# A mixture-of-experts tail that scatters its tokens to sorted rows, against one that gathers each tile inside the loop

## The chip, the cores and the metric

The kernel runs on one core of a Trainium2 chip. The time is that of the device in microseconds, the median of three runs: 3569.94 us (3564.78 to 3572.04). Engines are named as the profile names them: PE (TensorE), DVE (VectorE), ACT (ScalarE), POOL (GpSimd) and SP (SyncE). SP does no arithmetic here; it issues transfers. POOL issues transfers too, the indirect ones (gathers and scatters by a list of rows) among them.

## The reference

One decoder layer on x of 4 x 1024 tokens of width 256, in fp32. Every part adds to x and normalises:

```
x = layernorm(x + attn(x))      # a Mamba block twice (state 16, inner 512), then a decaying memory
x = layernorm(x + xattn(x, ctx))  # 16 heads over 64 context rows
x = layernorm(x + ffn(x))       # the part that the change is about

ffn(x):  logits = x @ Wg + bg                       # 8 experts
         top2, idx = top_k(logits, 2); scores = softmax(top2)
         y_e = gelu(x @ W1[e] + b1[e]) @ W2[e] + b2[e]   # hidden 1024
         out = sum over the two chosen e of score * y_e
         return layernorm(x + out) * gamma + beta
```

## The kernel before, in words

The five engines run own instruction streams and wait on each other by counting semaphores. The first three quarters of the time are the scan of the Mamba blocks and, in two groups of two batches, memory and cross-attention (xattn). At the end of xattn a batch's result (x2, 8 tiles of 128 tokens, 1 MB) stands in `x2_out`, which is also the place of the last batch in `x2`. SP stores batches 0 to 2 in `x2_dram` (`keep_x2`) as they are done.

The expert part begins when the last layer norm is done (`ln_done`). SP loads batch 0 (`x2_first`) and batches 1 and 2 (`x2_middle`). PE turns x2 (`turn_x2`, drained by ACT) and forms the logits (`logits`), for batches 0 and 3 first, then for 1 and 2. DVE routes: the two largest of 8 logits, one-hot selections, a count of the tokens ahead of each by two matrix products with `below` and `ones`, and from these `slot`, the row of each (token, choice) in a list sorted by expert. Each expert's part of the list begins on a tile of 128 rows (`bound`, in tiles). With 4096 tokens and two choices there are at least `FEWEST` = 64 tiles and at most `TILES` = 80; here there are 70.

When `slot` is known (`routed`), POOL issues 64 indirect stores (2 choices x 32 tiles of tokens), which write rows of x2 to `xs_dram` in sorted order. When all have landed (`xs_sorted`), SP loads the first sorted tile into `tile_in`. `xs_dram` is filled with zeros at the very start of the kernel, as are the upper tiles of `ys_dram`, so that rows without a token are defined.

The tile loop runs over expert pairs and, in each expert, over its tiles. One pass of PE does: the first product (two halves of 512 columns) of tile i+1; the transposes of tile i's hidden values (`turn_hidden`); the transposes of tile i+2 from `tile_in` (`turn_tile`); the second product of tile i. DVE adds b1 and b2 and copies turned values, ACT does gelu and drains. SP, in a loop of its own, waits until tile i+1 has been turned (`tileT_full`) and loads the next into the same `tile_in`; there is one such buffer. POOL (`keep_results`) waits for tile i's result (`y_ready`) and stores it in `ys_dram`; after the last tile of an expert it issues the four loads of the weights of the expert after next (`load_expert`, 2.6 MB) into the buffer that has come free. The first two experts' weights are issued right after `ln_done`.

At the end POOL gathers each token's two results from `ys_dram` by `slot`, and DVE weighs, adds and normalises, batch by batch.

`alone(engine)` is a step without work that separates two waits from the instruction after them. The transfers of one issuing engine stand in one queue: q1 in the profile for SP, q0 for POOL.

Of the kernel before, what the change touches and what calls it, by code (L numbers as in the profile page):

```python
# [38 lines left out]
def decoder_layer(nc, x, ctxT, ctx_mask, norm1_w, norm2_w, in_wT, in_b, conv_w, conv_b, xp_wT, dt_wT, dt_b,  # L39
# [57 lines left out]

    with ExitStack() as ctx:
# [11 lines left out]
        x2_dram = nc.dram_tensor("x2_dram", (NT - TT, P, D), F32, kind="Internal").ap()  # L110

        xs_dram = nc.dram_tensor("xs_dram", ((TILES + 1) * P, D), F32, kind="Internal").ap()
# [50 lines left out]
        WORDS = 41552  # L163
# [68 lines left out]
        tile_in = carve(D)  # L232
# [7 lines left out]
        tileT = carve(KD * P).rearrange("p (k t) -> p k t", k=KD)  # L240

# [3 lines left out]

        hid, act_hid = small[:, 0:HID], small[:, HID:2 * HID]
# [10 lines left out]
        steps_i = read_w_sb[:, 1, :].bitcast(I32).rearrange("p (e j) -> p e j", e=E)  # L257
        count = read_w_sb[:, 0, 0:E]
# [84 lines left out]
        xs_sorted = sem("xs_sorted")  # L343
# [132 lines left out]
        batch_order = [0, B - 1] + list(range(1, B - 1))  # L476
# [34 lines left out]
        ZEROED = 16 * (-(-(TILES + 1) // 4) + (TILES - FEWEST) // 4)  # L511
# [16 lines left out]
        def _(sp):  # L528
# [30 lines left out]
            for g0 in range(GROUPS):  # L559
# [22 lines left out]
                for u in range(2):  # L582
# [22 lines left out]
            sp.dma_start(x2[:, 0:TT, :], x2_dram[0:TT].rearrange("t p d -> p t d")).then_inc(x2_first, 16)  # L605
            sp.dma_start(x2[:, TT:NT - TT, :], x2_dram[TT:NT - TT].rearrange("t p d -> p t d")).then_inc(x2_middle, 16)

            sp.wait_ge(xs_sorted, 16 * 2 * NT)
            sp.wait_ge(routed, 1)
            sp.dma_start(tile_in, xs_dram[0:P, :]).then_inc(xs_loaded, 16)  # L610
            tiles = sp.value_load(bound[0:1, E:E + 1], min_val=FEWEST, max_val=TILES)
            with sp.Fori(0, tiles) as i:

                sp.wait_ge(tileT_full, i + 2)
                sp.wait_ge(xs_loaded, i * 16 + 16)
                alone(sp)
                sp.dma_start(tile_in, xs_dram[bass.ds(i * P + P, P), :]).then_inc(xs_loaded, 16)
# [1266 lines left out]
```

## Time and profile before

| | |
|---|---|
| median of 3 runs (lowest, highest) | 3569.94 us (3564.78, 3572.04) |
| profiled execution, its own time | 3567.79 us |
| its span | 3566.3 us |
| busy: PE, DVE, ACT, POOL | 2779.7, 2334.9, 1927.0, 1731.7 us |
| chain that ended last, by engine | PE 49%, DVE 21%, ACT 12%, issue 12%, POOL 4%, DMA 2% |
| last layer norm of xattn done | 2682.4 us after the start |
| first tile of the loop turned | 2825.6 us |
| last tile of the loop turned | 3402.4 us |

Times in the rows are microseconds from the start of the span. "Busy" is the time in which an engine executed an instruction; the chain is followed back from the last instruction, each step to what released it. A step of the chain called "issue" is time for which no releaser is visible in the records.

### The profile page before, as it was taken

The page shows a single profiled execution, that of the slowest core. Times are in us where ns is not written, and L with a number is a line of the kernel's source. Part 1 is how long each engine was busy: PE and PEld are TensorE (multiplying, and loading weights), DVE is VectorE, ACT ScalarE, POOL GpSimd, SP SyncE. Part 2 cuts the span into 40 slices and gives each one's busy share as a digit, 9 for nine tenths or more (in the row PEclk, how much of TensorE's full clock was granted, in tenths as well). Part 3 has the DMA queues.
Part 4 walks back from the last instruction along what each step waited for, and adds up shares of the span by engine and source line. Part 5 has one row for each costly group of instructions (what it writes and reads, how often), then busy time and mean ns, then how long its engine had stood idle before and what let it go on. Part 6 is the DMA issues. An engine that isn't in the chain of part 4 may idle for free.

```text
span 3566.3 us, 45643 instructions
## 1 busy us (share of the span) xinstructions
PE 2779.7 (78%) x15274; PEld 2049.3 (57%) x15275; DVE 2334.9 (65%) x3190; ACT 1927.0 (54%) x3239; POOL 1731.7 (49%) x1807
## 2 busy tenths in 40 slices
PE   3888788888887995788788888888993299999920
PEld 1666566666675653566666666665663166666610
DVE  3888988988882445988988888872442033333348
ACT  4877887887771335887887787771331012112100
POOL 1777767777781102777777776771102501000052
PEclk8998999999999997999999999998996699999965
DMA  6110111111111100111111111111003112111022
GB/s 226 31 37 30 37 34 33 34 36 39 40 45 53 36 1 24 36 34 33 33 37 33 34 34 42 39 39 42 24 1 123 78 64 93 62 63 63 32 76 72
DMA packets 100973, 171.52 MB, mean 48 GB/s; under 512 B 14514, under 2 KB 52658, under 8 KB 100786
## 3 DMA queue, kind: packets, MB, share of 16 engines
q1 hardware_dynamic: 82066, 119.38, 10.7%
q0 software_dynamic: 15392, 47.99, 3.6%
q8 instruction: 105, 1.72, 0.2%
q10 hardware_dynamic: 3328, 1.76, 0.2%
q14 instruction: 82, 0.67, 0.1%
HBM read 126.75 MB, written 42.34 MB: 47 GB/s over the span
## 4 chain that ended last, share of the span: by engine, by line
PE 49%; DVE 21%; ACT 12%; issue 12%; POOL 4%; DMA 2%; SPq 1%; another core or an unknown queue 0%; DVEq 0%; POOLq 0%; ACTq 0%; PEld 0%
PE psD L1062 17%; DVE arena L1587 8%; PE psD L1385 7%; PE psD L1160 6%; PE psA L1179 4%; ACT arena L910 4%; ACT arena L900 2%; POOL arena L709 2%; PE psD L1262 2%; PE psA L1237 2%; PE psA L1062 2%; PE psD L1283 2%; PE psA L1376 1%; PE psA L1169 1%; DVE arena L1576 1%
## 5 line engine op out<-in xcount | busy, mean ns | idle before, releaser
L709 POOL TENSOR_TENSOR arena<-arena 128x512 f32<-128x512 f32 x1024 | 1154.2, 1153 | 17.8 <-DVE arena L1587 7.3
L1160 PE MATMUL psD<-ident,arena 128*128 128x128 f32 x4096 | 691.1, 295 | 339.0 <-DVE arena L1587 309.7
L1160 PEld LDWEIGHTS psD<-ident,arena 128*128 128x128 f32 x4096 | 485.2, 148 | 601.9 <-DVE arena L1587 369.0
L910 ACT ACTIVATE arena<-arena,negA 128x512 f32<-128x512 f32 x1024 | 718.8, 711 | 25.2 <-DVE arena L1587 24.5
L1587 DVE TENSOR_TENSOR_SCAN arena<-arena,carry,psD 128x512 f32<-128x512 f32 x512 | 642.1, 1269 | 83.6 <-PE psA L1179 67.8
L1587 DVE TENSOR_TENSOR_SCAN arena<-arena,psD 128x512 f32<-128x512 f32 x512 | 612.9, 1208 | 93.3 <-PE psA L1179 75.8
L1179 PE MATMUL psA<-ident,arena 128*128 128x128 f32 x4096 | 650.2, 284 | 0.0
L900 ACT ACTIVATE arena<-arena,bc 128x512 f32<-128x512 f32 x768 | 545.9, 711 | 115.3 <-PE psD L1160 114.5
L1179 PEld LDWEIGHTS psA<-ident,arena 128*128 128x128 f32 x4096 | 514.6, 149 | 2.1 <-issue 2.1
L693 POOL TENSOR_SCALAR arena<-arena,bc 128x512 f32<-128x512 f32 x256 | 182.7, 714 | 464.1 <-PE psD L1160 400.3
L1062 PE MATMUL psD<-arena 128*128 128x512 f32 (+4 forms) x776 | 335.2, 567 | 46.4 <-POOL strip L653 31.6
L1019 ACT ACTIVATE in_w_sb<-in_w_sb 128x512 f32<-128x512 f32 x140 | 88.1, 629 | 456.4 <-DVE in_w_sb L1766 456.4
L759 POOL DMA_DIRECT2D ys_dram<-arena x70 | 38.1, 544 | 531.8 <-DVE arena L1777 524.1
L802 ACT ACTIVATE arena<-psA 128x512 f32<-128x512 f32 x160 | 90.8, 597 | 307.7 <-PE psA L1237 117.2
L1766 DVE TENSOR_TENSOR in_w_sb<-psD,arena 128x512 f32<-128x512 f32 x140 | 96.8, 692 | 244.6 <-PE psD L1062 244.6
L1385 PE MATMUL psD<-arena 128*128 128x256 f32 x1120 | 254.2, 380 | 2.9 <-DVE arena L1772 2.9
L1062 PE MATMUL psD<-arena,in_w_sb 128*128 128x512 f32 x512 | 242.7, 597 | 6.6 <-DVE halo L1546 4.9
L1062 PEld LDWEIGHTS psD<-arena 128*128 128x128 f32 (+1 forms) x776 | 142.2, 193 | 152.9 <-issue 143.2
L1385 PEld LDWEIGHTS psD<-arena 128*128 128x128 f32 x1120 | 207.3, 190 | 30.1 <-DVE arena L1772 4.8
L1535 DVE SCALAR_TENSOR_TENSOR arena<-psD,conv_w_sb,arena 128x511 f32<-128x511 f32 (+2 forms) x192 | 140.1, 730 | 51.7 <-ACT arena L856 51.1
L1777 DVE TENSOR_TENSOR arena<-psD,arena 128x256 f32 x70 | 29.7, 424 | 217.1 <-PE psD L1385 217.1
L731 POOL TENSOR_TENSOR arena<-arena 128x2048 f32<-128x2048 f32 x4 | 18.1, 4516 | 312.0 <-DMA arena<-in_x 312.0
(214 smaller groups left out, 3723.0 us busy)
## 6 DMA issues: line engine op xcount, KB each, us to landing
arena<-c_dram SPq DMA_DIRECT2D x256, 256.0 KB, 3.2
arena<-in_W POOLq DMA_DIRECT2D x16, 1024.0 KB, 7.5
xs_dram<-arena SPq DMA_DIRECT2D x20, 512.0 KB, 9.4
arena<-xs_dram SPq DMA_DIRECT2D x71, 128.0 KB
ys_dram<-arena POOLq DMA_DIRECT2D x70, 128.0 KB, 2.0
arena<-in_x SPq DMA_DIRECT2D x8, 1024.0 KB, 7.2
o_dram<-arena SPq DMA_DIRECT2D x32, 128.0 KB, 1.7
arena<-o_dram SPq DMA_DIRECT2D x4, 1024.0 KB, 5.6
```

What stands on the lines that cost most here:

```text
L693: pool.tensor_scalar(g[:, v % 2, JS, :], uT[:, i % 2, JS, :], bc[:, i % 2, JS, n:n + 1], 1.0, ALU.mult, ALU.mult).then_inc(b_by_pool, 1)
L709: pool.tensor_tensor(h_ring[:, c % H_SLOTS, :], h_ring[:, c % H_SLOTS, :], c_rows[:, v % C_SLOTS, :], ALU.mult).then_inc(c_weighed, 1)
L802: act.activation(dst, psA[:, bank, 0:width], func, **kw).then_inc(act_drained, 1)
L900: act.activation(g[:, v % 2, j, :], uT[:, i % 2, j, :], ACT.Copy, scale=bc[:, i % 2, j, n:n + 1])\
L910: act.activation(da_ring[:, c % DA_SLOTS, :], dt[:, i % 2, f, :], ACT.Exp, scale=negA[:, f, n:n + 1]).then_inc(da_ready, 1)
L1062: mm = pe.matmul(out_ap, lhs, rhs, start=i == 0, stop=i == len(pairs) - 1)
L1160: mm = pe.transpose(psD[:, c % FILL_BANKS, j * P:(j + 1) * P], g[:, (c // KI) % 2, j, c % KI * P:(c % KI + 1) * P], ident[:, :])
L1179: mm = pe.matmul(psA[:, f, j * P:(j + 1) * P], h_ring[:, c % H_SLOTS, j * P:(j + 1) * P], ident[:, :], is_transpose=True, start=False, sto ...
L1385: mm = pe.matmul(psD[:, 2, 0:D], hidT[:, k, :], w2_sb[:, r, k, :], start=k == 0, stop=k == KH - 1)
L1535: last = dve.scalar_tensor_tensor(xm[:, f, cols:], bank[:, 0:HALF - cols], conv_w_sb[:, f, tap:tap + 1], xm[:, f, cols:], op0=ALU.mult, op ...
L1587: dve.tensor_tensor_scan(h_ring[:, c % H_SLOTS, :], da_ring[:, c % DA_SLOTS, :], psD[:, c % FILL_BANKS, :], 0.0 if h == 0 else carry[:, u, ...
L1766: dve.tensor_tensor(hid[:, n * BANK:(n + 1) * BANK], psD[:, n, :], b1_sb[:, r, n * BANK:(n + 1) * BANK], ALU.add).then_inc(hid_ready, 1)
```

## The change

Nothing is scattered. The sorted order is kept as a list of token numbers, `token_of`, with one column for each tile of 128 rows: entry (p, i) is the token in row p of tile i. It is made from the slots by matrix products. Each slot is split into its tile number (`slot_hi`) and its row in the tile (`slot_lo`). For each of the 64 groups of 128 (token, choice) pairs DVE makes a one-hot matrix of the row (128x128) and one of the tile, scaled by the token's number (128x83), and PE adds up the 64 products in one bank of PSUM. Rows without a token get number 0, so they hold token 0's values.

Three columns (`LEAD`) are gathered before the loop and one in each pass, by POOL: it copies the column of `token_of` to a fixed place, `token_now`, since the indirect transfer takes its list from a fixed address, then gathers 128 rows of `x2_dram` into `stage`, and SP moves `stage` to `tile_in`. All four batches are now kept in `x2_dram`. Batches 0 and 1 are fetched back to `x2` during xattn of the last two batches, only batch 2 after it, and the order of the batches is 0, 1, 3, 2. The zeroing of `xs_dram` goes.

```diff
-        x2_dram = nc.dram_tensor("x2_dram", (NT - TT, P, D), F32, kind="Internal").ap()
-
...
-        batch_order = [0, B - 1] + list(range(1, B - 1))
+        batch_order = [0, 1, 3, 2]
...
-            rows = xs_dram.rearrange("(p r) d -> p (r d)", p=P)
-            for c in range(-(-(TILES + 1) // 4)):
-                lo, hi = c * 4 * D, min((c + 1) * 4 * D, (TILES + 1) * D)
-                sp.dma_start(rows[:, lo:hi], zeros[:, 0:hi - lo]).then_inc(xs_zeroed, 16)
...
                     if b + 2 < B:
                         sp.dma_start(xin[:, u, :, :], x[b + 2].rearrange("(t p) d -> p t d", p=P)).then_inc(x_loaded[u], 16)
+                    else:
+                        sp.wait_ge(x2_stored, 16 * (u + 2))
+                        sp.dma_start(x2[:, u * TT:(u + 1) * TT, :], x2_dram[u * TT:(u + 1) * TT].rearrange("t p d -> p t d"))\
+                          .then_inc(x2_first, 16)
...
             sp.wait_ge(x2_stored, 16 * B)
             sp.wait_ge(ln_done, B * 2 * TT)
-            sp.dma_start(x2[:, 0:TT, :], x2_dram[0:TT].rearrange("t p d -> p t d")).then_inc(x2_first, 16)
-            sp.dma_start(x2[:, TT:NT - TT, :], x2_dram[TT:NT - TT].rearrange("t p d -> p t d")).then_inc(x2_middle, 16)
-
-            sp.wait_ge(xs_sorted, 16 * 2 * NT)
+            sp.dma_start(x2[:, 2 * TT:3 * TT, :], x2_dram[2 * TT:3 * TT].rearrange("t p d -> p t d")).then_inc(x2_middle, 16)
+            keep_x2(B - 1)
+
             sp.wait_ge(routed, 1)
-            sp.dma_start(tile_in, xs_dram[0:P, :]).then_inc(xs_loaded, 16)
+            sp.wait_ge(gathered, 16)
+            sp.dma_start(tile_in, stage).then_inc(xs_loaded, 16)
...
-            with sp.Fori(0, tiles) as i:
+            with sp.Fori(0, tiles + 1) as i:
 
                 sp.wait_ge(tileT_full, i + 2)
                 sp.wait_ge(xs_loaded, i * 16 + 16)
                 alone(sp)
-                sp.dma_start(tile_in, xs_dram[bass.ds(i * P + P, P), :]).then_inc(xs_loaded, 16)
+                sp.wait_ge(gathered, i * 16 + 32)
+                sp.dma_start(tile_in, stage).then_inc(xs_loaded, 16)
...
+            pool.iota(column_i, pattern=[[1, P]], base=0, channel_multiplier=0).then_inc(steps_ready, 1)
+            pool.iota(token_i, pattern=[[P, NT]], base=0, channel_multiplier=1).then_inc(steps_ready, 1)
             for e in range(2):
                 load_expert(pool, e, e)
-            pool.wait_ge(x2_first, 16)
-            pool.wait_ge(x2_middle, 16)
-            pool.wait_ge(routed, 1)
-            for r in range(2):
-                for t in range(NT):
-                    pool.indirect_dma_start(xs_dram, bass.IndirectOffsetOnAxis(slot[:, r, t:t + 1], 0), x2[:, t, :], None)\
-                        .then_inc(xs_sorted, 16)
+
+            pool.wait_ge(x2_stored, 16 * (B + 1))
+            pool.wait_ge(dve_drained, END_D + 7 + RING)
+            x2_rows = x2_dram.rearrange("t p d -> (t p) d")
+            for i in range(LEAD):
+                if i >= 1:
+                    pool.wait_ge(xs_loaded, 16 * i)
+                pool.indirect_dma_start(stage, None, x2_rows, bass.IndirectOffsetOnAxis(token_of[:, i:i + 1], 0))\
+                    .then_inc(gathered, 16)
...
                 first, end = expert_tiles(pool, e)
                 with pool.Fori(first, end) as i:
+                    pool.wait_ge(xs_loaded, i * 16 + 16 * LEAD)
+                    alone(pool)
+                    pool.dma_start(token_now, token_of[:, bass.ds(i + LEAD, 1)]).then_inc(token_moved, 16)
+                    pool.wait_ge(token_moved, i * 16 + 16)
+                    alone(pool)
+                    pool.indirect_dma_start(stage, None, x2_rows, bass.IndirectOffsetOnAxis(token_now, 0)).then_inc(gathered, 16)
                     pool.wait_ge(y_ready, i + 2)
                     alone(pool)
                     pool.dma_start(ys_dram[bass.ds(i * P, P), :], ys[:, bass.ds(i, 1), :].rearrange("p o d -> p (o d)"))\
...
-            pe.wait_ge(x2_first, 16)
-            turn_x2(0)
-            turn_x2(B - 1)
-            logits(0)
-            logits(B - 1)
-            pe.wait_ge(x2_middle, 16)
-            for q in range(1, B - 1):
+            pe.wait_ge(x2_first, 32)
+            for j, q in enumerate(batch_order):
+                if q == 2:
+                    pe.wait_ge(x2_middle, 16)
                 turn_x2(q)
-            for q in range(1, B - 1):
-                logits(q)
+                if j >= 1:
+                    logits(batch_order[j - 1])
+            logits(batch_order[B - 1])
...
+            claim_d(END_D + 6)
+            for n in range(2 * NT):
+                if n % 16 == 0:
+                    pe.wait_ge(one_hot, (n // 16 + 1) * 17)
+                mm = pe.matmul(psD[:, (END_D + 6) % RING, 0:TILES + LEAD], one_lo[:, n, :], one_hi[:, n, :],
+                               start=n == 0, stop=n == 2 * NT - 1)
+            mm.then_inc(dve_full, 1)
...
+
+
+            place_of = rest[:, 5:7, :].rearrange("p r t -> p (r t)")
+            link(dve.tensor_scalar(scaled, place_of, 1.0 / P, -(P - 1) / (2.0 * P), ALU.mult, ALU.add))
+            link(dve.tensor_scalar(scaled, scaled, ROUNDER, None, ALU.add))
+            link(dve.tensor_scalar(slot_hi, scaled, ROUNDER, None, ALU.subtract))
+            link(dve.tensor_scalar(slot_lo, slot_hi, float(P), None, ALU.mult))
+            link(dve.tensor_tensor(slot_lo, place_of, slot_lo, ALU.subtract))
+            for c in range(2 * NT // 16):
+                dve.tensor_tensor(one_lo[:, 16 * c:16 * c + 16, :], column.unsqueeze(1).broadcast_to([P, 16, P]),
+                                  slot_lo[:, 16 * c:16 * c + 16].unsqueeze(2).broadcast_to([P, 16, P]), ALU.is_equal)\
+                   .then_inc(one_hot, 1)
+                for n in range(16 * c, 16 * c + 16):
+                    dve.tensor_scalar(one_hi[:, n, :], column[:, 0:TILES + LEAD], slot_hi[:, n:n + 1], token[:, n % NT:n % NT + 1],
+                                      ALU.is_equal, ALU.mult).then_inc(one_hot, 1)
+            dve.wait_ge(dve_full, END_D + 7)
+            dve.tensor_copy(token_of, psD[:, (END_D + 6) % RING, 0:TILES + LEAD]).then_inc(dve_drained, 1)
```

The buffers: `tile_in` and `stage` are the two halves of `write_w_sb`, `token_now` is a column of `read_w_sb`, and the one-hot matrices lie in the place of `ys`, which is not in use before the loop.

## Rows read from the trace of the kernel before

**Rows 1.** The page: DMA share in tenths, in 40 slices of 89 us.

```profile
DMA  6110111111111100111111111111003112111022
```

**Rows 2.** The chain that ended last: start us, length us, what.

```profile
2679.75 2.68 DVE arena L1494 x8
...
2682.50 0.38 SPq L605
...
2682.92 24.93 DMA arena<-x_dram
...
2731.08 95.23 issue
```

**Rows 3.** The timeline of the logits: start us, busy us, engine, line, operation.

```profile
2688.10 5.51 PE L1319 MATMUL psA<-ident,arena 128*128 128x128 f32 x32 [11.80 <-issue]
...
2702.37 0.22 DVE L1702 TENSOR_TENSOR in_w_sb<-psD,bg_sb 128x64 f32<-128x64 f32 x1 [5.03 <-PE psD L1062]
...
2707.90 5.85 PE L1319 MATMUL psA<-ident,arena 128*128 128x128 f32 x32 [5.57 <-DMA arena<-x_dram]
...
2722.21 0.22 DVE L1702 TENSOR_TENSOR in_w_sb<-psD,bg_sb 128x64 f32<-128x64 f32 x1 [4.72 <-PE psD L1062]
```

**Rows 4.** The timeline from the slots to the first tile.

```profile
2739.78 0.20 DVE L1759 CAST slot<-out_w_sb 128x64 uint32<-128x64 f32 x1
2740.93 1.05 POOL L750 DMA_INDIRECT xs_dram<-arena,slot  x1 [52.03 <-DVE slot L1759]
2742.28 1.00 POOL L750 DMA_INDIRECT xs_dram<-arena,slot  x1 [0.30 <-issue]
...
2823.27 0.36 SPq L610 DMA_DIRECT2D arena<-xs_dram  x1
...
2825.61 0.66 PE L1355 MATMUL psA<-ident,arena 128*128 128x128 f32 x2 [92.53 <-DMA arena<-xs_dram]
```

**Rows 5.** The timeline of one steady pass of the tile loop.

```profile
2847.79 0.38 PE L1355 MATMUL psA<-ident,arena 128*128 128x128 f32 x2
...
2851.79 0.42 DVE L1777 TENSOR_TENSOR arena<-psD,arena 128x256 f32 x1 [3.04 <-PE psD L1385]
...
2853.10 0.56 POOL L759 DMA_DIRECT2D ys_dram<-arena  x1 [7.31 <-DVE arena L1777]
...
2855.77 0.38 PE L1355 MATMUL psA<-ident,arena 128*128 128x128 f32 x2
```

**Rows 6.** The chain behind the last tile: start us, length us, what.

```profile
3412.61 1.95 DMA ys_dram<-arena
...
3414.60 0.88 issue
...
3434.40 2.69 DMA arena<-ys_dram,slot
```

**Rows 7.** DMA issues of two small stores by SP: count, KB, us to landing.

```profile
o_dram<-arena SPq DMA_DIRECT2D x32, 128.0 KB, 1.7
...
c_dram<-arena SPq DMA_DIRECT2D x16, 32.0 KB, 1.6
```

**Rows 8.** The chain where the second expert starts.

```profile
2923.89 0.23 PE psA L1355 x2
...
2924.45 6.29 DMA arena<-xs_dram
...
2930.78 0.44 PE psA L1355 x2
```

**Rows 9.** The timeline: instructions near in kind to the new ones.

```profile
2661.01 1.87 PE L1283 MATMUL psD<-arena 128*128 128x34 f32 x16
...
2679.75 2.67 DVE L1494 TENSOR_SCALAR arena<-arena,aggr,rs 128x256 f32<-128x256 f32 x8
...
2722.47 2.27 DVE L1717 MAX8 in_w_sb<-in_w_sb 128x8 f32<-128x8 f32 x32
...
3460.96 2.29 DVE L1831 TENSOR_TENSOR arena<-arena,gamma_sb 128x2048 f32<-128x2048 f32 x1 [7.08 <-remote]
```

More of the change, by code:

```diff
@@ L96, in decoder_layer @@
     STEPS = B * T // P
+    ROUNDER = 1.5 * 2.0 ** 23
+    LEAD = 3
     with ExitStack() as ctx:
@@ L109, in decoder_layer @@
         o2_dram = nc.dram_tensor("o2_dram", (2, TT, P, D), F32, kind="Internal").ap()
-        x2_dram = nc.dram_tensor("x2_dram", (NT - TT, P, D), F32, kind="Internal").ap()
-        xs_dram = nc.dram_tensor("xs_dram", ((TILES + 1) * P, D), F32, kind="Internal").ap()
+        x2_dram = nc.dram_tensor("x2_dram", (NT, P, D), F32, kind="Internal").ap()
         ys_dram = nc.dram_tensor("ys_dram", (TILES * P, D), F32, kind="Internal").ap()
@@ L160, in decoder_layer @@
         rsum = sb("rsum", [P, 2, HEADS])
-        WORDS = 41552
+        WORDS = 41560
         arena = sb("arena", [P, WORDS])
@@ L231, in decoder_layer @@
         ys_flat = ys.rearrange("p t d -> p (t d)")
-        tile_in = carve(D)
         x2T = ys_flat[:, 0:NT * D].rearrange("p (k t) -> p k t", k=KD)
@@ L240, in decoder_layer @@
         tileT = carve(KD * P).rearrange("p (k t) -> p k t", k=KD)
+        token_of = carve(TILES + LEAD).bitcast(U32)
+        one_lo = ys_flat[:, 0:2 * NT * P].rearrange("p (n c) -> p n c", c=P)
+        one_hi = ys_flat[:, 2 * NT * P:2 * NT * (P + TILES + LEAD)].rearrange("p (n c) -> p n c", c=TILES + LEAD)
         small = in_w_sb[:, :, :].rearrange("p k f -> p (k f)")
         small2 = out_w_sb[:, :, :].rearrange("p k f -> p (k f)")
+        tile_in, stage = write_w_sb[:, 0, :], write_w_sb[:, 1, :]
+        token_now = read_w_sb[:, 1, 0:1].bitcast(U32)
         hid, act_hid = small[:, 0:HID], small[:, HID:2 * HID]
@@ L257, in decoder_layer @@
         steps_i = read_w_sb[:, 1, :].bitcast(I32).rearrange("p (e j) -> p e j", e=E)
+        slot_hi, slot_lo, scaled = (top_words.rearrange("p t e -> p (t e)")[:, 0:2 * NT] for top_words in (top, topf, sel1))
+        column_i, column = wq_sb[:, 0, 0:P].bitcast(I32), wq_sb[:, 1, 0:P]
+        token_i, token = wo_sb[:, 0, 0:NT].bitcast(I32), wo_sb[:, 1, 0:NT]
         count = read_w_sb[:, 0, 0:E]
@@ L342, in decoder_layer @@
         xs_zeroed = sem("xs_zeroed")
-        xs_sorted = sem("xs_sorted")
+        gathered = sem("gathered")
+        token_moved = sem("token_moved")
+        one_hot = sem("one_hot")
         xs_loaded = sem("xs_loaded")
@@ L510, in decoder_layer @@
         LOADED = 16 * len(loads)
-        ZEROED = 16 * (-(-(TILES + 1) // 4) + (TILES - FEWEST) // 4)
+        ZEROED = 16 * ((TILES - FEWEST) // 4)
         def load_expert(engine, e, r):
@@ L1732, in _ @@
             link(dve.tensor_tensor(rest[:, 4, :], rest[:, 1, :], rest[:, 3, :], ALU.mult))
-            dve.wait_ge(steps_ready, 1)
+            dve.wait_ge(steps_ready, 3)
             link(dve.tensor_copy(steps, steps_i))
+            link(dve.tensor_copy(column, column_i), wait=False)
+            link(dve.tensor_copy(token, token_i))
             for j, dst in enumerate((place, total)):
```

2 lines of the change are left out of this document (1 added, 1 removed).

## The prediction

> **What bounds the kernel now.** I read the page first, then the chain that ended last, then timelines of the three stretches that the diff touches. The first 2,682 us (scan, memory, cross-attention) are left alone but for one early transfer. Behind them the chain shows two holes. One is 24.93 us for one load of x2, the other is 95.23 us of "issue" [rows 2]. The second hole runs to the first tile: the slots are ready at 2739.98, POOL then issues 64 scatters, one every 1.3 us, SP loads tile 0 at 2823.27, and PE turns it at 2825.61 [rows 4]. From there 70 tiles run in a loop whose steady pass is 2855.77 - 2847.79 = 7.98 us, PE busy throughout [rows 5]. So there is a front part, where a wait is worth its full length, and a loop, where anything shorter than 7.98 us per tile is free and anything longer is paid 70 times.
>
> **The change, part by part.** Baseline is the profiled execution, 3567.8 us (span 3566.3), 2.1 us under the median of the three runs and inside their scatter.
>
> *a. The x2 fetch.* x2 is complete at 2679.75 + 2.68 = 2682.43 [rows 2]. The logits now come in two halves, 2688.10 to 2702.59 and 2707.90 to 2722.43, 14.5 us each, the second behind the 2 MB load [rows 3]. The last logit is in at +40.0 us. Afterwards batches 0 and 1 are already in SBUF and batch 3 is where it was written, so PE starts at +0.1 and has three batches to turn before it wants batch 2. That load is 1 MB, issued at +0.07 ahead of the expert weights on POOL, as the first 1 MB is now, which was there by 2688.10 [rows 3]. I take the two halves back to back, 29.0 us, last logit at +29.1, 2711.5: **-10.9 us**. Only the gap between the halves and the wait ahead of the first go, not all of 24.93, since half the work was inside it. Bounds: if each of the 192 matmul instructions in it took the 0.117 us of the small ones [rows 9], the stretch would be 22.5 us and the gain 17.4; if batch 2 landed only at 2707.9, as the 2 MB load does now [rows 3], with a quarter of the work (7.3 us) behind it, the last logit would be at 2715.2 and the gain 7.2. The two fetches in cross-attention run where the DMA engines are at 1 tenth or less [rows 1], behind waits that SP has passed by then. I cost them at nothing: no engine waits on SP there, and if they met another transfer it would be some 5 us each. The third store of x2 (1 MB) ends long before the first gather, under the routing.
>
> *b. Zeroing.* 21 stores of zeros at the start go. They stand behind all weight loads on SP's queue, and nothing in the chain waits for them: 0. Bound: a few us less if they slow loads.
>
> *c. Routing and one-hots.* Last logit to slots is 2739.98 - 2722.43 = 17.55 us [rows 3, 4]; two more copies add 0.45. Then new DVE work, none of it covered: 5 small operations at 0.24 (1.2 us); 4 comparisons of 128x2048, each 2.29 as L1831 (9.2 us); 64 operations of 128x83 with two scalar columns. Of those no row has the width: eight wide ones (256) take 2.67, 0.334 each, and 8-wide ones 2.27 / 32 = 0.071 each [rows 9], so 0.071 + 75 x 0.00106 = 0.15, 9.6 us. DVE: 20.0 us. The 128 matmul instructions (64 products, two instructions each in fp32) go along by groups of 32; 16 of 34 columns take 1.87, 0.117 each [rows 9], and with 83 columns, on a PE that has idled, I take 0.145, 4.6 us a group, just under DVE's 4.7. Only the last group shows. With the copy out of PSUM (0.35) token_of is ready 20.0 + 4.6 + 0.35 = 25.0 us after the slots, say 25.2. Bounds: 24 (PE faster) and 36.7 (0.33 for each narrow operation).
>
> *d. First tile.* POOL wakes 0.95 us after its releaser (2739.98 to 2740.93 [rows 4]); the gather takes 2.69 from issue to landing, as the gathers of the results do [rows 6]; SP starts 0.07 to 0.12 after its releaser (2682.43 to 2682.50 [rows 2]); then the move from stage to tile_in. SBUF to SBUF of 128 KB has no row. Bounds: 1.7, a store of the same size by SP [rows 7], and 2.3, the tile load of now with PE's wake-up (2823.27 to 2825.61 [rows 4]); I take 2.0. First turn at 2711.5 + 18.0 + 25.2 + 0.95 + 2.69 + 0.12 + 2.0 = 2760.5, where it now is 2825.6. With a: **-65.1 us** (bounds -50, both dear ends together, and -73). From the slots to the first turn it is 85.6 us now and 31 us then.
>
> *e. The loop.* This is the term that decides. The old load for the next tile needed only the previous turn and 2.3 us. The new one is a ring of three transfers. There is one stage, so POOL may start on tile k only when tile k-1 has been moved out of it: copy of the token column, gather, move by SP, and only then the next. Length P of one round:
> POOL wakes after a landing and forms an address with a register, 0.87 (2851.79 + 0.42 to 2853.10 is 0.89 [rows 5]); the token copy, 128 rows of 4 bytes, 1.8; POOL wakes for the indirect one, 0.92 (landing 3414.56 to 3415.48 [rows 6]); gather 2.69 [rows 6]; SP 0.12; move 2.0. **P = 8.40 us**, against a pass of 7.98.
> The token copy has no row. Bounds: 1.6, the 32 KB store by SP [rows 7], and 1.95, POOL's 128 KB store [rows 6]; I take 1.8, since most of either is not data. With all bounds together P is 7.4 (gather at a plain load's 2.3) to 9.4 (gather 3.0, one gap of 0.30 between POOL's transfers [rows 4] more; SP 0.33), and the loop from about +1 to +96.
> POOL's other duties fit: behind the gather's issue it waits for the result of tile i, then issues the store (0.56) and is back before the move lands. That wait queues nothing else on POOL but the next token copy. The result of pass i comes 4.3 us after turn i+2, just as the gather's issue ends, so POOL is free at 6 of 8.4 us.
> I stepped this tile by tile: turn k = later of (move k landed) and (turn k-1 + PE's own gap); move k starts at the later of gather k and turn k-1; gather k follows move k-1. At each of the seven later experts' starts PE has two first products in a row between two turns, more than P, and the ring catches up; the first two turns are PE's too. So about 61 turns pay P - 7.98. The six loads of weights come in ahead: a tile load inside such a load takes 6.29 rather than 2.3 [rows 8]. Before, PE's work hid nearly all of it (turn to turn 2924.12 to 2930.78); in the ring all but some 1.6 us each, 9.5 together. The token copy waits on POOL's queue behind the weights, but these land about when the copy would anyway. Loop: 61 x 0.42 + 9.5 = **+35.1 us**.
>
> *f. Tail.* The last gathers issue before the last result is added; the picks of the results are as before: 0.
>
> **Sum:** 3567.8 - 65.1 + 35.1 = 3537.8, and I say 3538 us.
>
> **Rivals.**
> 1. *The ring is hidden (P at or under 8.05).* Then only the boundaries cost, +3 to +14, and the time is 3506 to 3517. For it: 1.7 for the move and 1.6 for the copy give 7.9. Against: the tile load, also rows of 1 KB into SBUF, took 2.3, and all other legs would have to keep their times too. Chance 0.2.
> 2. *The ring eats the gain.* P = 8.75 to 9.0 gives +56 to +72, within 0.2% of now: 3559 to 3575. For it: it is the sum with the dear bounds of move and copy. Chance 0.1.
> 3. *The token copy is dear.* One mechanism: 128 writes of 4 bytes by POOL's queue, if they cost as much as the gather (2.69, its nearest indirect relative), make P = 9.29 and the loop +89.4: 3592 us, slower. It decides from a copy of about 2.4 us on (P = 9.0). Against it: the stores' 1.6 to 1.95 are mostly fixed. Chance 0.2, which takes in the case that gather or wake-ups are longer by as much. The Trainium skill (DMA: Bandwidth & Descriptors, Specifications) says that below 512 bytes the DMA engine does read-modify-write and loses line rate; by it the copy is the kind of transfer that runs dearer than its size, which is this rival's direction. No row here shows a 4-byte write into SBUF.
> 4. *The one-hots are dear* (0.33 each, so 53.6 gained in place of 65.1): this only shifts the forecast by 11 us and is in the range.
>
> **How the numbers follow.** The forecast, P from 8.05 to 8.75, has 0.5 and by itself spans 3517 to 3562 with c's bounds. A run tells nothing from no change within 0.2%, 7 us. Faster: 0.5 + 0.2 = 0.70; same 0.10; slower 0.20. The range reaches down to the hidden ring and up into rival 3: 3507 to 3583 leaves out about 2 in 10.
>
> **What the profile after would show.** First turn of a tile near 2760; last logit near 2711; DVE 20 us behind the slots. In the loop: turn to turn 8.4 us rather than 7.98 away from expert starts, PE waiting there for a DMA into tile_in, and SP waiting for the gather, not for PE. If the pass is still 7.98 us, rival 1 holds; if it is over 9, rival 3, and the times of its three legs say which. I am wrong if the token copy lands well off 1.8 us, if the move is off 2.0, or if the one-hot stretch is far from 25 us.

## The result, and the profile after

| | before | after |
|---|---|---|
| median of the timed runs, us | 3570.99 (3564.78 to 3577.25, 4 runs) | 3535.34 (3523.03 to 3548.59, 4 runs) |
| ratio, 95% interval | | 0.989 [0.9867, 0.9913] |
| profiled execution, us (span) | 3567.8 (3566.3) | 3548.59 (3546.8) |

The kernel became 1.1% faster, 35.7 us by the medians, and 3535.34 stands 2.7 us from the 3538 on record. The profiled execution after was the slowest of its four runs and shows only 19.5 us. Timed again on another chip the same kernel ran in 3518.84 us against 3548.78 us, ratio 0.9918 [0.9902, 0.9935], 29.9 us. The total was met; its terms were not. The front part (from the complete x2 to the first turn of a tile) gained 46.6 us where 65.1 were promised, and the loop (from the first turn to the last) gave back 17.6 where 35.1 were feared. The two errors have opposite signs and cancel within 1 us, which is luck.

The front part, in the timeline of PE after (start us, busy us, engine, line, operation):

```profile
2681.76 6.59 PE L1340 MATMUL psA<-ident,arena 128*128 128x128 f32 x32 [6.17 <-DVE arena L1521]
2688.18 4.16 PE L1083 MATMUL psD<-wg_sb,arena 128*128 128x8 f32 x32
2692.20 3.65 PE L1340 MATMUL psA<-ident,arena 128*128 128x128 f32 x16
2695.64 6.83 PE L1083 MATMUL psD<-wg_sb,arena 128*128 128x8 f32 x32
...
2705.78 13.66 PE L1083 MATMUL psD<-wg_sb,arena 128*128 128x8 f32 x64
...
2744.50 27.57 PE L1374 MATMUL psD<-arena 128*128 128x83 f32 x128 [14.15 <-DVE arena L1802]
2778.29 0.66 PE L1382 MATMUL psA<-ident,write_w_sb 128*128 128x128 f32 x2 [6.22 <-DMA write_w_sb<-write_w_sb]
```

The x2 wait is gone: PE starts 0.05 us behind the complete x2 (2681.71) and runs four batches without a hole. But it is slow at it. The logits of the first batch take 4.16 / 32 = 0.130 us for an instruction, all later ones 6.83 / 32 = 0.213. The windows of that stretch say why (us, busy and count of each engine, granted clock, DMA share, GB/s):

```profile
2682.00:2690.00 8.00, 8.00 (x49) 8.00 (x49) 0.00 (x0) 4.68 (x8) 6.17 (x11) 0.64 0.84 260
2690.00:2700.00 10.00, 10.00 (x55) 10.00 (x54) 0.22 (x1) 2.40 (x4) 0.00 (x0) 0.56 1.04 411
2700.00:2720.00 20.00, 19.44 (x92) 19.34 (x92) 0.94 (x7) 3.68 (x5) 0.00 (x0) 0.50 0.18 72
2744.00:2772.00 28.00, 27.50 (x128) 27.38 (x128) 18.15 (x53) 0.00 (x0) 0.00 (x0) 0.50 0.00 1
```

Granted clock 0.50 is the level of 1.2 GHz, and PE is at it from 2700 through the token product to the first tile. Before, two windows of the same work had:

```profile
2690.00:2700.00 10.00, 10.00 (x79) 10.00 (x78) 0.23 (x1) 3.81 (x7) 0.00 (x0) 0.84 1.03 402
2710.00:2720.00 10.00, 10.00 (x79) 10.00 (x77) 0.23 (x1) 5.05 (x8) 0.00 (x0) 0.84 0.01 2
```

79 instructions in 10 us before, 46 to 55 after. Two shorter stretches of before show that its clock, too, falls while PE is busy with the logits:

```profile
2692.00:2698.00 6.00, 6.00 (x57) 6.00 (x55) 0.23 (x1) 2.40 (x5) 0.00 (x0) 1.00 1.03 392
2699.00:2702.00 3.00, 3.00 (x16) 3.00 (x16) 0.00 (x0) 0.00 (x0) 0.00 (x0) 0.50 1.03 412
```

Before had such a stretch at 1.00 in either half (the second from 2713 to 2719, 57 instructions again); after has one of 3 us (2688 to 2691, 30 instructions) and none behind it. The last logit is in at +38.0 us, where [rows 2, 3] gave +40.0. The one-hots, in the timeline of DVE, POOL and SP after:

```profile
2737.05 0.20 DVE L1788 CAST slot<-out_w_sb 128x64 uint32<-128x64 f32 x1
...
2738.33 2.29 DVE L1798 TENSOR_TENSOR arena<-wq_sb,in_w_sb 128x2048 f32<-128x2048 f32 x1
2740.54 3.82 DVE L1802 TENSOR_SCALAR arena<-wq_sb,in_w_sb,wo_sb 128x83 f32<-128x83 f32 x16
...
2758.33 3.82 DVE L1802 TENSOR_SCALAR arena<-wq_sb,in_w_sb,wo_sb 128x83 f32<-128x83 f32 x16
2772.11 0.24 DVE L1805 CAST arena<-psD 128x83 uint32<-128x83 f32 x1 [9.96 <-PE psD L1374]
2773.19 1.04 POOL L765 DMA_INDIRECT write_w_sb<-x_dram,arena  x1 [85.00 <-DVE arena L1805]
2776.04 0.54 SPq L620 DMA_DIRECT2D write_w_sb<-write_w_sb  x1
```

The slots are ready at 2737.25, 17.55 us behind the last logit as before [rows 3, 4]. From there DVE takes 24.9 us, and PE another 10.0 behind it.

The loop, in the chain that ended last, one steady round of the ring after (start us, length us, what):

```profile
3306.54 1.64 DMA read_w_sb<-arena
...
3308.98 2.78 DMA write_w_sb<-x_dram,read_w_sb
...
3311.78 2.06 DMA write_w_sb<-write_w_sb
...
3314.56 1.62 DMA read_w_sb<-arena
```

A round is copy 1.64, wake 0.80 (POOL, until it issues the gather), gather 2.78, hand-over to SP 0.02, move 2.06, wake 0.72: 8.02 us. The transfers by kind, in the DMA issues of a window (count, KB, us to landing):

```profile
write_w_sb<-write_w_sb SPq DMA_DIRECT2D x6, 128.0 KB, 2.0
write_w_sb<-x_dram,read_w_sb POOLq DMA_INDIRECT x6, 2.8
read_w_sb<-arena POOLq DMA_DIRECT2D x5, 0.5 KB, 1.6
```

And the passes are not 8.4 us long: 41 of the 70 intervals between turns are the 7.98 or 7.99 of [rows 5], as were 50 before. From first turn to last it is 594.32 us (2778.29 to 3372.61) where it was 576.75. The rest is lost in a few passes behind each expert's start, here the second expert's, in the chain after:

```profile
2877.68 0.23 PE psA L1382 x2
...
2878.15 6.66 DMA write_w_sb<-write_w_sb
...
2885.56 2.95 DMA read_w_sb<-arena
...
2889.30 2.87 DMA write_w_sb<-x_dram,read_w_sb
...
2894.88 1.62 DMA read_w_sb<-arena
```

A move of 6.66 us, started as a load of weights begins, and a copy of 2.95. With 6.29 for the tile load there [rows 8] the size is the same, but now the next copy, gather and move stand behind it. The passes there are 12.07, 7.34, 9.34, 8.14 us; before they were 12.06, 7.06, 8.04, 7.98. Behind another load of weights it is the token copy that waits, since it stands behind them in POOL's queue:

```profile
2982.87 5.70 DMA read_w_sb<-arena
```

It took 4.27 us behind the fifth load. The two passes behind the 5.70, with a move of 6.65 us in the next load, are 10.86 and 10.67 us, where they were 6.77 and 8.04.

The first pass has another cause. It takes 8.87 us, and 7.76 before; the windows over it, before and after:

```profile
2825.00:2835.00 10.00, 6.48 (x12) 2.80 (x12) 1.39 (x2) 2.93 (x5) 0.00 (x0) 0.66 0.05 13
2778.00:2788.00 10.00, 7.56 (x12) 3.10 (x12) 1.26 (x2) 2.30 (x3) 1.94 (x2) 0.57 0.13 39
```

The granted clock rises to 1.00 only 8.4 us behind the first turn, before it was 6.2 us, and the pass is longer by half of the difference. The kernels below agree: 6.9 us and a pass of 8.13 with all turns first, 8.5 us and 8.95 with the x2 fetch alone. So the first pass is paid to the clock and not to the ring.

### The profile page after: what moved, and what is told of

It is laid out like the page before. It is cut to its first block, busy times and chain, and to the rows that moved or that the text cites. A ratio compares the mean times of both kernels' runs of the same rounds, so it can differ in the third digit from the quotient of the medians.

```text
span 3546.8 us, 46325 instructions
## 1 busy us (share of the span) xinstructions
PE 2817.5 (79%) x15402; PEld 2084.2 (59%) x15403; DVE 2358.7 (67%) x3266; ACT 1928.5 (54%) x3239; POOL 1775.1 (50%) x1888
## 4 chain that ended last, share of the span: by engine, by line
PE 42%; DVE 23%; ACT 13%; issue 11%; DMA 9%; POOL 1%; SPq 0%; another core or an unknown queue 0%; POOLq 0%; DVEq 0%; ACTq 0%
PE psD L1083 14%; DVE arena L1614 9%; PE psD L1181 6%; PE psA L1200 5%; ACT arena L931 4%; DMA write_w_sb<-x_dram,read_w_sb 4%; DMA write_w_sb<-write_w_sb 3%; ACT arena L921 3%; PE psD L1412 3%; DMA read_w_sb<-arena 2%; PE psD L1283 2%; PE psA L1083 2%; PE psA L1258 2%; PE psA L1190 2%; PE psD L1304 2%
## 5 line engine op out<-in xcount | busy, mean ns | idle before, releaser
L1614 DVE TENSOR_TENSOR_SCAN arena<-arena,psD 128x512 f32<-128x512 f32 x512 | 612.9, 1208 | 93.4 <-PE psA L1200 75.6
L1812 DVE TENSOR_TENSOR in_w_sb<-psD,arena 128x512 f32<-128x512 f32 x140 | 96.8, 691 | 166.0 <-PE psD L1083 166.0
L777 POOL DMA_INDIRECT write_w_sb<-x_dram,read_w_sb x70 | 69.6, 995 | 141.6 <-DMA read_w_sb<-arena 134.1
```

The lines of the kernel that those rows point to most:

```text
L1614: dve.tensor_tensor_scan(h_ring[:, c % H_SLOTS, :], da_ring[:, c % DA_SLOTS, :], psD[:, c % FILL_BANKS, :], 0.0 if h == 0 else carry[:, u, ...
L1812: dve.tensor_tensor(hid[:, n * BANK:(n + 1) * BANK], psD[:, n, :], b1_sb[:, r, n * BANK:(n + 1) * BANK], ALU.add).then_inc(hid_ready, 1)
```

## The experiments

Times of a kernel are compared with the kernel before on the same chip (3548.78, 3547.05 and 3548.60 us in the three groups), and stretches with stretches of the profiles. "Front" is from the complete x2 to the first turn of a tile, "loop" from first turn to last, "tail" from there to the end of the span.

| kernel | median us | ratio to before, 95% | front | loop | tail |
|---|---|---|---|---|---|
| before (first chip's profile) | 3570.99 | | 143.2 | 576.8 | 163.9 |
| after (first chip's profile) | 3535.34 | 0.989 [0.9867, 0.9913] | 96.6 | 594.3 | 174.2 |
| after, again | 3518.84 | 0.9918 [0.9902, 0.9935] | 96.7 | 593.8 | 148.1 |
| no token copy | 3504.88 | 0.9874 [0.9854, 0.9893] | 96.7 | 582.7 | 147.4 |
| token copy twice | 3670.69 | 1.0354 [1.0331, 1.0377] | 96.7 | 742.3 | 155.5 |
| after, no weight loads | 3497.64 | 0.986 [0.9841, 0.9878] | 96.7 | 576.4 | 149.4 |
| before, no weight loads | 3542.11 | 0.999 [0.9981, 1.0] | 143.0 | 574.9 | 147.3 |
| x2 fetch alone | 3544.99 | 0.9997 [0.9986, 1.0007] | 140.8 | 579.0 | 147.2 |
| bf16 one-hots | 3508.84 | 0.9895 [0.9879, 0.9912] | 86.6 | 593.5 | 149.6 |
| gathered ahead | 3504.17 | 0.9877 [0.9861, 0.9894] | 96.8 | 582.2 | 147.4 |
| both of these | 3494.13 | 0.9854 [0.9835, 0.9873] | 86.7 | 581.4 | 147.2 |
| PE busy ahead of the product | 3520.44 | 0.9923 [0.9903, 0.9943] | 93.4 | 591.1 | 149.8 |
| all turns first | 3519.21 | 0.9918 [0.9898, 0.9939] | 94.7 | 592.7 | 149.7 |

**The change again.**

> The changed kernel once more, five rounds, for its scatter. Its four runs so far lie 25 us apart (3523 to 3549) and its profile was the slowest of them. If the scatter is in the ring of the loop and in the tail (gathers that take 3.7 us rather than 2.8, idle stretches of the normalisation), a profile of a faster run shows the same front (first turn within 3 us of 2778.3) and a shorter loop and tail than 594.3 and 174.2 us. If it is in the front (how long PE stays at 1.2 GHz), the loop and tail keep these lengths and the first turn moves by 10 us or more. Median 3530 to 3545.

The median, 3518.84 us, lies under the range given. Front and loop kept their lengths, and the first turn moved 3.9 us only because x2 was complete 4.0 us earlier. What moved is the tail, 174.2 to 148.1 us. Two rows of DVE's normalisation in the first profile of after:

```profile
3423.27 2.67 DVE L1863 TENSOR_SCALAR arena<-arena,strip 128x256 f32<-128x256 f32 x8 [1.57 <-remote]
3432.39 2.29 DVE L1877 TENSOR_TENSOR arena<-arena,gamma_sb 128x2048 f32<-128x2048 f32 x1 [6.46 <-remote]
```

and the same two in the second:

```profile
3414.43 2.77 DVE L1863 TENSOR_SCALAR arena<-arena,strip 128x256 f32<-128x256 f32 x8
3417.24 2.29 DVE L1877 TENSOR_TENSOR arena<-arena,gamma_sb 128x2048 f32<-128x2048 f32 x1
```

Six holes (idle time of DVE) of 1.5 to 7 us, 24.6 together, that no work of the program explains, stand in the first profile, five, 17.3 us, in the kernel before's on the same chip (one of them the 7.08 of [rows 9]), and none of 1 us or more in any of the profiles on other chips. The holes differ by 7.3 of the 10.3 us by which the tail looked longer. Without any, it is 148.1 us here and 147.2 in a variant of the kernel before (the x2 fetch alone, below). So the 10.3 us are no cost of the change, but for 1 us at most. The expectation that a faster run has a shorter loop as well fell.

**No token copy.**

```diff
-                    pool.dma_start(token_now, token_of[:, bass.ds(i + LEAD, 1)]).then_inc(token_moved, 16)
-                    pool.wait_ge(token_moved, i * 16 + 16)
-                    alone(pool)
-                    pool.indirect_dma_start(stage, None, x2_rows, bass.IndirectOffsetOnAxis(token_now, 0)).then_inc(gathered, 16)
+                    pool.indirect_dma_start(stage, None, x2_rows, bass.IndirectOffsetOnAxis(token_of[:, LEAD:LEAD + 1], 0)).then_inc(gathered, 16)
```

> The change without the copy of the token column in the loop: every gather of the loop takes the rows named by one fixed column, so that all its tiles hold the same tokens; every other instruction is there. It takes some 2.4 us out of the ring (copy 1.6, wake-up 0.8), which then lasts 5.6 us against a pass of 7.98. Theory: the ring, 8.0 us long in the profile after, has no slack, and what delays it once (a load of weights, a slow gather) is paid to the end; with slack it is caught up. Then the loop from first to last turn takes 577 us (574 to 582) in place of 594.3, and the time falls by 12 to 20 us. Rival: the 17.6 us come from PE and from contention of the weights with the tile load alone, whatever the ring's length: loop 590 to 597, time within 4 us of the change's. With 5.6 us the prediction's own model gives the loop of the kernel before too.

The loop fell by 11.1 us to 582.7, and the time by 14.0. The rival (590 to 597) fell. The theory is met in the main; its 577 was 5.7 too low, just outside its range, and the last sentence on the model fell with it: an expert's first passes stay at 7.5 to 8 us, though the ring is 2.4 us shorter. The edit also takes away a transfer that waits behind the weights in POOL's queue (the 5.70 us above), so the 11.1 us are shown to belong to the copy, but not how much of them is slack and how much is this wait.

**Token copy twice.**

```diff
+                    pool.wait_ge(token_moved, i * 32 + 16)
+                    alone(pool)
+                    pool.dma_start(token_now, token_of[:, bass.ds(i + LEAD, 1)]).then_inc(token_moved, 16)
+                    pool.wait_ge(token_moved, i * 32 + 32)
```

> The change with its token copy made twice in a row, each waited for. It adds one wake-up and one copy, 2.4 us, to the ring: 8.0 + 2.4 = 10.4 us. Theory that the ring is the bound: nearly every pass lasts 10.4 us and the loop some 743 us in place of 594 (+150 us, 135 to 165); the few passes at an expert's start, longer than that by themselves, give it a little back. Rival, that PE's 7.98 us is the bound and the ring has some slack of 1 us or more: at most +90 us. It also gives the price of one copy with its wake-up, for the prediction's third rival: 2.4 us if the profile's legs hold.

+151.9 us in time, the loop 742.3, as expected for the ring as the bound; the steady pass is 10.1 us rather than 10.4. With the ring as the bound its own legs can be read in the chain:

```profile
3324.93 1.62 DMA read_w_sb<-arena
...
3327.16 1.64 DMA read_w_sb<-arena
...
3329.60 2.75 DMA write_w_sb<-x_dram,read_w_sb
3332.37 1.93 DMA write_w_sb<-write_w_sb
...
3335.00 1.63 DMA read_w_sb<-arena
```

A round is 10.07 us, and the second copy with its wake-up is 3327.16 - 3324.93 = 2.23 of it. Without it 7.84 us are left: the ring's own length, 0.14 us under the pass of 7.98. That is one round. Rounds of the changed kernel away from the loads of weights last from 7.80 to 8.04 us, the one shown above 8.02, so its slack is some 0.1 us or less, and nothing in some rounds.

**No weight loads, after and before.** The same edit in either kernel (here after; before has its own line number):

```diff
-                    load_expert(pool, pair * 2 + (r + 2), r)
+                    load_little(pool, pair * 2 + (r + 2), r)
```

> The change with the weights of experts 2 to 7 not loaded: in the place of each load stand four stores of 16 KB on the same queue, and these experts are computed with the weights of experts 0 and 1. Theory: most of the loop's surplus over the kernel before (17.6 us) comes from the six loads, which delay gather or move by some 2 to 4 us each in a ring without slack; the loop is 576 to 583 us in place of 594.3, the time 10 to 18 us lower. Rival: the surplus comes from the ring's own length and from slow gathers; the loop stays within 4 us of 594.

> The kernel before with the weights of experts 2 to 7 not loaded (four stores of 16 KB on the same queue in the place of each load; these experts are computed with the weights of experts 0 and 1): the partner of the same edit on the kernel after, whose loop fell from 593.8 to 576.4 us by it. Theory: a load of weights costs much only where the ring behind it has no slack; here the tile load needs 2.3 us of a pass, so the loop of 577 us falls by 2 to 4 us (the surplus of the passes behind the experts' starts, 6.6 to 7.1 us where 6.44 is the shortest) and so does the time. Rival: the loads slow PE's own operands or the tile load by 17 us in either kernel: the time falls by 12 to 20 us.

Loops of 576.4 after and 574.9 before. These four loops settle where the time goes: with the loads 593.8 and 576.8, without them 576.4 and 574.9. The change without the loads costs 1.5 us: 0.9 in the first pass, which is the clock (it rises 8.3 us behind the first turn, against 6.3), and the rest in one pass of 8.51 us with a gather of 3.71 rather than 2.8. The loads alone, with the old tile load, cost 1.9. Both together cost 18.9, so 15.5 us belong to their meeting. A tile load of 6.29 us was nearly absorbed before, since it otherwise used 2.3 us of a pass; the ring can absorb some 0.1.

The time of the first fell by 21.2 us, more than expected: 17.4 are in the loop, and x2 was complete 5.6 us earlier, in a part that the edit does not touch. The time of the second fell by 4.9 us, with 1.9 in the loop. Both rivals fell.

**The x2 fetch alone.**

> The kernel before with part a of the change alone: batches 0 and 1 fetched back in cross-attention, the four batches turned in the order 0, 1, 3, 2. What the prediction put on it was -10.9 us (7.2 to 17.4). The profile after shows the four batches without a wait but at the lower clock, last logit at +38.0 us behind the complete x2, where the kernel before has +40.0. Theory: it is worth 2 to 3 us, the last logit 37 to 38 us behind the last part of x2, with a granted clock near 0.55 in that stretch. Rival: the lower clock came with the rest of the change; here the last logit is at +29 us and the time falls by 9 to 12 us. Where this chip's last stretch has no idle holes in the normalisation, as the kernel after had none in its second profile, this kernel shows from last turn to end 146 to 149 us; else 160 or more.

Last logit at +38.0 us, front shorter by 2.4, ratio 0.9997: nothing that the time can show. From this profile's timeline of PE:

```profile
2679.26 4.16 PE L1065 MATMUL psD<-wg_sb,arena 128*128 128x8 f32 x32
...
2686.72 6.83 PE L1065 MATMUL psD<-wg_sb,arena 128*128 128x8 f32 x32
```

The same 0.130 and 0.213 us as in the whole change. The tail without holes is 147.2 us, beside 148.1 of the changed kernel: the change costs it 1 us at most.

**All turns first.**

```diff
-            for j, q in enumerate(batch_order):
-                if q == 2:
-                    pe.wait_ge(x2_middle, 16)
-                turn_x2(q)
-                if j >= 1:
-                    logits(batch_order[j - 1])
-            logits(batch_order[B - 1])
+            for q in batch_order[:B - 1]:
+                turn_x2(q)
+            for q in batch_order[:B - 1]:
+                logits(q)
+            pe.wait_ge(x2_middle, 16)
+            turn_x2(batch_order[B - 1])
+            logits(batch_order[B - 1])
```

> The change with PE's order in the x2 stage as it was before it: batches 0, 1 and 3 all turned first (96 transposes), then their logits, then batch 2. In the profiles after, logits instructions of 8 columns take 0.130 us for the first batch and 0.213 us for all later ones, the granted clock being 0.50 from some 12 us on; before, with a pause of 5 us for the load between two halves, it was 0.84 right after the pause. Theory: the long run of 8-column products is what the clock falls in, whatever order they stand in: here too some two thirds of the logits run at 0.21 us, last logit 36 to 38 us behind the complete x2, time within 2 us of the changed kernel's. Rival: the mixed order (turn a batch, logits of the one before) lets the clock fall: last logit at 30 to 33 us, 5 to 8 us gained.

Last logit at +36.0, front 2.0 us shorter, time as the changed kernel's (0.9918 both). Not the order of turns and logits, then. 96 logits instructions in 16.30 us here, 0.170 each, the last 32 in 6.97 (0.218), at 0.64 and then 0.50 of the clock. That the pause of 5 us raised the clock before was not tried by itself; the clock is 0.50 for the first 4 us behind it and 1.00 only then, and the mean of 0.84 holds these and the fall within the logits.

**PE busy ahead of the token product.**

```diff
             claim_d(END_D + 6)
+            for n in range(40):
+                pe.matmul(psD[:, (END_D + 6) % RING, 0:256], ident[:, :], gamma_sb[:, :], start=True, stop=True)
             for n in range(2 * NT):
```

> The change with 40 idle-time products on PE (128x256 fp32, identity by gamma, into the bank that the first token product clears) between the two prefix sums and the wait for the first group of one-hots, where PE is idle for 14 us. Nothing else is touched. Theory: the 0.215 us of a token-number instruction (predicted 0.145) are the lower clock level, 0.50 of full in the records; work in front of them raises it, the 128 instructions take 0.12 to 0.15 us each, PE waits for VectorE's groups again, and behind the last group stand 4 to 5 us in place of 10: first turn 90 to 92 us behind the complete x2 in place of 96.5, the time 4 to 6 us lower. Rival: the instructions take 0.215 us at any clock (weight loads or reading fp32 sets them): nothing gained, or 1 to 4 us lost if the added products run past the first group.

PE's timeline:

```profile
2732.47 18.38 PE L1372 MATMUL psD<-gamma_sb,ident 128*128 128x256 f32 x80
2750.69 7.27 PE L1376 MATMUL psD<-arena 128*128 128x83 f32 x64
2758.61 3.80 PE L1376 MATMUL psD<-arena 128*128 128x83 f32 x32 [0.65 <-DVE arena L1804]
2764.54 6.63 PE L1376 MATMUL psD<-arena 128*128 128x83 f32 x32 [2.13 <-DVE arena L1804]
```

and its windows, as above:

```profile
2751.00:2758.00 7.00, 6.96 (x63) 6.81 (x61) 7.00 (x23) 0.00 (x0) 0.00 (x0) 1.00 0.01 2
2758.00:2763.00 5.00, 3.80 (x32) 3.65 (x32) 5.00 (x15) 0.00 (x0) 0.00 (x0) 1.00 0.00 0
2764.00:2771.00 7.00, 6.46 (x32) 6.41 (x32) 0.49 (x3) 0.00 (x0) 0.00 (x0) 0.58 0.00 0
```

At clock 1.00 the same instruction takes 0.114 to 0.119 us, at 0.58 it takes 0.207. So the 0.215 of the changed kernel is the clock, and the rival fell. But the level was lost again for the group that is exposed (the clock falls 0.6 us into it), after waits of 0.65 and 2.13 us, so that the front is 3.3 us shorter rather than 4 to 6, and the time shows nothing (0.9923 to 0.9918). The Trainium skill (TensorE: Matmul & The Clock Gate, Part 1) says that PE has its full clock once it has been busy, and half of it when idle. The added products agree. The logits stretch does not: PE is busy for 19.44 of 20 us in the records (2700 to 2720 above) and is at 0.50.

**bf16 one-hots.** The token number is split into tile and partition, so that both halves are exact in bf16; 64 products of 168 columns, one instruction each.

```diff
-                mm = pe.matmul(psD[:, (END_D + 6) % RING, 0:TILES + LEAD], one_lo[:, n, :], one_hi[:, n, :],
+                mm = pe.matmul(psD[:, (END_D + 6) % RING, 0:2 * COLS], one_lo[:, n, :], one_hi[:, n, :, :].rearrange("p h c -> p (h c)"),
...
-                for n in range(16 * c, 16 * c + 16):
-                    dve.tensor_scalar(one_hi[:, n, :], column[:, 0:TILES + LEAD], slot_hi[:, n:n + 1], token[:, n % NT:n % NT + 1],
-                                      ALU.is_equal, ALU.mult).then_inc(one_hot, 1)
+                dve.tensor_tensor(same_hi[:, part, :], column[:, 0:COLS].unsqueeze(1).broadcast_to([P, 16, COLS]),
+                                  hi_lo[:, 0, part].unsqueeze(2).broadcast_to([P, 16, COLS]), ALU.is_equal).then_inc(same_step, 1)
```

> The change with its one-hots in bf16: token number split into tile and partition (two halves of 84 columns), comparisons for 16 columns of tokens at a time on VectorE, the second half scaled by ScalarE, and 64 products in one pass in place of 64 in two. Theory: behind VectorE's last one-hot the profile after shows 10.0 us of PE (128 instructions of 0.215 us at the lower clock) where the prediction had 4.6; 16 single instructions are left behind it here, 2 to 4 us. VectorE's own part is 4 x (2.3 + 2 x 1.5) = 21 us, as now, or less if bf16 runs faster. First turn 6 to 15 us earlier behind the complete x2 (80 to 90 us in place of 96.5), and the time lower by as much. Rival: VectorE is the bound and PE's tail is hidden by what follows: 0 to 2 us.

```profile
2739.03 2.40 PE L1388 MATMUL psD<-arena 128*128 128x168 bf16 x16 [13.64 <-DVE arena L1822]
...
2754.40 2.42 PE L1388 MATMUL psD<-arena 128*128 128x168 bf16 x16 [2.71 <-DVE arena L1822]
2763.31 0.66 PE L1396 MATMUL psA<-ident,write_w_sb 128*128 128x128 f32 x2 [6.48 <-DMA write_w_sb<-write_w_sb]
```

Front 86.6 us, 10.1 less than the changed kernel's. The time is 38.2 us under the kernel before on its chip, where the changed kernel was 29.9 under it on its own: 8.3 us more. PE waits for each group of DVE's, 5.13 us apart, and only 2.4 us stand behind the last.

**Gathered ahead.**

```diff
+            for grp, size in enumerate(SIZES):
+                for i in range(sum(SIZES[:grp]), sum(SIZES[:grp + 1])):
+                    pool.indirect_dma_start(ys[:, i, :], None, x2_rows, bass.IndirectOffsetOnAxis(token_of[:, i:i + 1], 0))\
+                        .then_inc(gathered[grp], 16)
...
-                sp.dma_start(tile_in, stage).then_inc(xs_loaded, 16)
+                sp.dma_start(tile_in, xs[:, bass.ds(i + 1, 1), :].rearrange("p o d -> p (o d)")).then_inc(xs_loaded, 16)
```

> The change without its ring: right behind the token numbers POOL gathers all 80 tiles into the slots in which the results stand later, with a fixed column each, and SP moves one slot to the operand tile in each pass; no copy of a token column, no stage, and the gathers run ahead of PE (one each 1.3 us against a pass of 7.98). Theory: with the ring gone the loop has the length that it had before, 576 to 579 us in place of 593.8, the first turn stands where it is now or 1 to 2 us later (the first gather is passed on by POOL behind the issue of the second), and the time is 14 to 18 us lower. Rival: 80 gathers in a row block POOL's queue, the first results and the third expert's weights come late and PE waits for them: the gain is under 8 us or gone, and the passes of the first two experts are longer than 7.98 us.

Loop 582.2, front as it was, 42.9 us under the kernel before on its chip, 12.9 more than the changed kernel; 14 to 18 were expected. The loop is 3 us above the range given, at the figure of the kernel without a token copy. Of the 5.4 us over the 576.8 of before 1.0 is the first pass. The rest stands at the experts' starts, where a move falls into a load of weights, as in the chain of this kernel at the third expert's start:

```profile
2950.62 7.74 DMA write_w_sb<-arena
...
2958.41 0.44 PE psA L1385 x2
```

**Both.**

> The two edits that each gained on the changed kernel together: one-hots in bf16 (first turn 10 us earlier behind the complete x2) and all tiles gathered ahead into the result slots in place of the ring (loop 582 in place of 594 us). Theory: one acts before the first turn and the other behind it, so that they add: first turn 86 to 88 us behind the complete x2, loop 580 to 584, 22 to 25 us under the changed kernel, ratio to the kernel before 0.984 to 0.986. Rival: they share something (POOL's row of gathers now starts while ScalarE and VectorE still run, or the weights of the first two experts are not yet there when the first turn comes 10 us earlier): under 15 us gained.

The gains add: front 86.7, loop 581.4, 54.5 us under the kernel before on its chip, 24.5 more than the changed kernel, ratio 0.9854 [0.9835, 0.9873]. It is the fastest that was run.

## Why the prediction was right, and where its terms were not

The number holds by luck, since two errors cancelled: -65.1 + 35.1 = -30.0 on record, -46.6 + 17.6 = -29.0 in the profiles, and -29.9 by the medians of the chip on whose changed kernel the tail had no holes.

*a.* "29.0 us for the two halves back to back", -10.9. The wait went as foreseen, and the gain was 2.0: logits 24.7 us of PE rather than 17.5, turns 13.9 rather than 11.4, 9.7 us given back. The failed step is the assumption that PE's durations stay when its pauses go. They belong to a granted clock of 0.84 in those windows, and without the pause it was 0.50. The lower bound of 7.2 did not hold it, since both bounds were made of durations at the clock of before.

*b.* Zeroing 0: x2 was complete at 2681.71 us after, 2682.43 before, and 2670.7 to 2684.0 in other profiles. Nothing shows a cost or a gain.

*c.* Routing 17.55 us: right. One-hots 25.2 on record, 35.1 measured, inside its bound of 36.7. Two sizes: the operation with two scalar columns took 0.239 us (3.82 for 16) rather than 0.15, which made DVE's part 24.9 rather than 20.0, and the last products 10.0 rather than 4.6, at 0.215 us rather than 0.145 an instruction. The first of these is interpolated from rows of another form; the second is the clock again.

*d.* 5.8 on record, 5.9 measured from token_of to the first turn, gather 2.79, move 2.0: right.

*e.* The ring was named rightly as the new danger of the loop, but it is not the bound of a steady pass, as the forecast had it: 41 of 70 passes keep the 7.98 us of PE. P is some 7.9 us, 7.84 in the round taken apart above, not 8.40: the copy 1.64 rather than 1.8, wake-ups 0.72 and 0.80 rather than 0.87 and 0.92, hand-over 0.02 rather than 0.12, gather 2.8, move 2.0. That is rival 1's condition, and the +17.6 lies above its "+3 to +14"; the term "61 passes x 0.42", 25.6 us, fell away whole. The 9.5 us for the starts of experts were too small, 15.5 by the four loops. The forecast counted one delayed move for each start, and had the token copy's wait behind the weights at nothing, where it took 5.70 and 4.27 us in two of the six. So the loop stands between rival 1 and the forecast.

*f.* Tail 0: right, within 1 us. Of the 10.3 us of the first profile 7.3 are the difference of the holes that both profiles of the first chip have.

Rival 2 needed P = 8.75 and fell. Rival 3, a copy as dear as a gather, fell too, at 1.64 us; that a second copy, 2.23 us more in the ring, cost 151.9 us shows that its direction was the real danger. The Trainium skill (DMA: Bandwidth & Descriptors, Specifications) has transfers below 512 bytes read, modify and write; the 128 writes of 4 bytes took no longer than the 32 KB store of [rows 7], 1.6 us, so that nothing of it shows here.

Left open: why PE's clock falls within the logits though the records show it busy, why it rises later behind the first turn with the new fetch, how the 15.5 us divide between the missing slack and the copy's wait in POOL's queue, and what the holes in the tail are.

## What to carry to other kernels

A ring of dependent transfers that is just as long as the pass cost 0.6 us here while nothing fell into it, and 15.5 us more once six loads of weights did: measure its slack (add a known leg, subtract it), then ask which transfers will hit it. A duration read next to a wait holds for the clock of that moment; where a change takes the wait away, cost the work at the lower level too. Two scattered terms that cancel are no proof of either: read front, loop and tail by themselves.

## What was not expected of the hardware

PE, busy for 19.44 of 20 us in the records with 8-column fp32 products and transposes, was at 0.50 of its clock there in every kernel with the new fetch; the kernel without it had 1.00 for 6 us in either half of the same work, and fell to 0.50 within the logits too. A 128 KB transfer from SBUF to SBUF took 2.0 us alone and up to 7.74 inside the 2.6 MB of an expert's weights. The copy of one 4-byte column took 1.64 us, as long as the 32 KB store of [rows 7]. The normalisation of one chip had up to 24.6 us of idle holes on DVE, that of the others none, with the same program.
